# Moving ScalarE's second normalization scaling from slot 3 to slot 5 of a row attention, and its store behind the value-row DMAs

## What is computed

```
projected = einsum('bte,fe->btf', query, in_proj_weight)      # q, k, v of 16 heads of 8
attention = einsum('bhtd,bhkd->bhtk', q / sqrt(8), k) + causal mask
x   = einsum('bhtk,bhkd->bhtd', softmax(attention), v)
out = einsum('bte,fe->btf', x, out_proj_weight)
x   = layernorm(x + out)        # (x - mean) / sqrt(var + 1e-5), no weights
```

## Time and profile before

| | us |
|---|---|
| Median of 3 runs (830.15 to 830.43) | 830.31 |
| The profiled execution, its own time | 829.71 |
| Its span | 828.0 |
| TensorE busy in the span | 577.7 (70%) |
| TensorE weight loads | 391.7 (47%) |
| VectorE | 465.2 (56%) |
| GpSimd | 405.4 (49%) |
| ScalarE | 321.6 (39%) |
| Mean granted TensorE clock | 0.83 of full |

### The profile page before, as it was taken

The page is one execution under the profiler, slowest core; times in us unless marked ns, Lnnn a source line. Parts: engine busy times, 40 slices in busy tenths (PEclk is TensorE's granted clock), DMA queues, the critical chain, the costliest instruction groups (busy, mean ns, idle before and its releaser), DMA issues. The chain is left out here.

```text
span 828.0 us, 16573 instructions
## 1 busy us (share of the span) xinstructions
PE 577.7 (70%) x5632; PEld 391.7 (47%) x5633; DVE 465.2 (56%) x1216; ACT 321.6 (39%) x685; POOL 405.4 (49%) x661
## 2 busy tenths in 40 slices
PE   2769788888888753899928888888411359878910
PEld 1335445445545332899915566656200236555610
DVE  1646666755766326455516899999587622222105
ACT  1035655565556720355514556564300021312105
POOL 7034544544454520544256588863240156777623
PEclk9978989988999955899967999999855556978665
DMA  4674656655530000222221111210100113434217
GB/s 115 139 172 91 144 117 124 125 111 109 108 70 16 15 13 1 58 67 70 55 65 39 40 53 52 68 44 28 51 8 0 41 44 58 86 62 87 23 16 203
DMA packets 72935, 57.69 MB, mean 70 GB/s; under 512 B 15608, under 2 KB 62624, under 8 KB 72864
## 3 DMA queue, kind: packets, MB, share of 16 engines
q1 hardware_dynamic: 64928, 47.72, 24.8%
q0 software_dynamic: 7936, 9.05, 6.3%
HBM read 36.95 MB, written 19.53 MB: 68 GB/s over the span
## 5 line engine op out<-in xcount | busy, mean ns | idle before, releaser
L578 DVE TENSOR_REDUCE a_mx<-a_psR 128x6 f32<-128x768 f32 x128 | 121.8, 954 | 65.6 <-PE a_psR L316 63.9
L245 POOL TENSOR_SCALAR_AFFINE_SELECT a_pr<-a_pr 128x512 f32<-128x512 f32 x128 | 81.3, 635 | 134.8 <-ACT a_pr L492 134.7
L492 ACT ACTIVATE a_pr<-a_psR 128x768 f32<-128x768 f32 x128 | 103.5, 810 | 86.6 <-PE a_psR L329 85.8
L756 POOL DMA_INDIRECT e_xt<-x1d,source x40 | 38.1, 952 | 54.9 <-PE e_psX L767 33.4
L1642 POOL DMA_INDIRECT acc<-e_ot,e_ixa x32 | 50.3, 1572 | 23.3 <-DVE e_ot L1682 11.8
L308 PE MATMUL a_psR<-a_maskA,identb 128*128 128x256 bf16 x256 | 54.0, 296 | 8.6 <-DMA a_ks<-qkd 8.0
L336 PE MATMUL a_psO<-a_pr,a_va 128*32 128x256 f32 x512 | 46.9, 442 | 3.8 <-ACT a_onT L484 2.1
L1707 ACT ACTIVATE e_hT<-e_psH,e_b 128x512 f32<-128x512 f32 x32 | 22.0, 687 | 70.6 <-PE e_psH L1727 69.4
L1743 PE MATMUL e_psY<-e_w,e_hT 128*128 128x128 f32 x256 | 46.6, 338 | 1.9 <-ACT e_hT L1707 1.9
L326 PE MATMUL a_psR<-a_qs,a_ks 50*128 50x256 bf16 x256 | 37.6, 291 | 14.2 <-DMA a_qs<-a_mlo 11.5
L1007 POOL TENSOR_TENSOR a_rs<-a_ve,mhalf 128x2 f32<-128x2 f32 x32 | 22.8, 711 | 47.9 <-DVE a_ve L1255 46.8
(11 more groups left out here) (296 smaller groups left out, 1434.0 us busy)
## 6 DMA issues: line engine op xcount, KB each, us to landing
qkd<-a_hml SPq DMA_DIRECT2D x16, 384.0 KB, 3.0
e_w<-in_fc SPq DMA_DIRECT2D x16, 256.0 KB
a_qs<-qkd SPq DMA_DIRECT2D x32, 96.0 KB
a_ks<-qkd SPq DMA_DIRECT2D x32, 96.0 KB
ys<-e_yt SPq DMA_DIRECT2D x40, 64.0 KB, 1.5
a_qs<-qkd SPq DMA_DIRECT2D x32, 64.0 KB
a_ks<-qkd SPq DMA_DIRECT2D x32, 64.0 KB
x1d<-a_x SPq DMA_DIRECT2D x16, 128.0 KB, 1.8
```

The lines of the kernel that those rows point to most:

```text
L245: g.affine_select(out=diagonal, in_=diagonal, pattern=[[0, 4], [1, 128]], compare_op=ALU.is_ge, fill=0.0, base=0, channel_multiplier=-1).t ...
L492: a.activation(pr[s][:, :, 0:3, :].rearrange("p x k q -> p x (k q)"), psR[:, r:r + 2, 0:384], ACT.Exp).then_inc(probs, 1)
L578: v.tensor_reduce(mx[b % 2][:, :, 2 * u:2 * u + 35:17], psR[:, r:r + 2, 0:384].rearrange("p x (k c) -> p x k c", c=128), AX.X, ALU.max).th ...
L756: pool.indirect_dma_start(xt[n % 4][:], None, x1d, bass.IndirectOffsetOnAxis(ap=source[:, n:n + 1], axis=0)).then_inc(x_in[n % 4], 16)
```

## The change

On ScalarE, the scaling of batch G stands behind the exp of slot 5 instead of slot 3. Within slots 4 and 5 it is thus passed by the copy of the values, the exp of slot 4, `mhi`, `onT` and the exp of slot 5. On SP, the wait for the scaling and the store of `x1` stand behind the four row DMAs and ahead of the stack loads, instead of ahead of the rows. Nothing else changes.

```
--- before.py
+++ after.py
@@ -192,9 +192,6 @@
                     sp.wait_ge(qk_high, P + 1)
                     sp.wait_ge(qk_low, P + 1)
                     sp.dma_start(qkd[P % 2].rearrange("c r f t -> f (c r) t"), hml[P % 2][:]).then_inc(hml_out[P % 2], 16)
-                if G is not None:
-                    sp.wait_ge(x1_sb, G + 1)
-                    sp.dma_start(x1v[G], x1[G % 2][:]).then_inc(x1_out[G % 2], 16)
                 if V is not None:
                     for parts, ready, a in ((mhi, mhi_sb, 0), (mlo, mlo_sb, 1)):
                         sp.wait_ge(ready, V + 1)
@@ -202,6 +199,9 @@
                             r = 64 * h + 48 + a
                             sp.dma_start(qs[V % NQ][r:r + 1], parts[V % 2][:, h, :]
                                          ).then_inc(rows_in[V % NQ], 16)
+                if G is not None:
+                    sp.wait_ge(x1_sb, G + 1)
+                    sp.dma_start(x1v[G], x1[G % 2][:]).then_inc(x1_out[G % 2], 16)
                 if P is not None:
                     sp.wait_ge(hml_out[P % 2], 16 * (P // 2 + 1))
                     if P >= NQ:
@@ -491,7 +491,7 @@
                         r = banks(probs, (B, s))
                         a.activation(pr[s][:, :, 0:3, :].rearrange("p x k q -> p x (k q)"), psR[:, r:r + 2, 0:384], ACT.Exp
                                      ).then_inc(probs, 1)
-                    if s == 3 and G is not None:
+                    if s == 5 and G is not None:
                         act.wait_ge(nr_sb, G + 1)
                         if G >= 2:
                             act.wait_ge(x1_out[G % 2], 16 * (G // 2))
```

## The result

| | Before | After |
|---|---|---|
| Median, us | 830.23 (827.54 to 830.43, now 4 runs) | 786.9 (783.59 to 788.36, 4 runs) |
| Profiled execution, us | 829.71 | 785.63 |
| Span, us | 828.0 | 783.8 |
| TensorE busy | 577.7 (70%) | 559.3 (71%) |
| Mean granted TensorE clock | 0.83 | 0.845 |

The ratio is 0.9489, with a 95% interval of 0.9452 to 0.9527. The direction was right, the size was not. The predicted gain was 33.9 us, the measured one 43.3 (44.2 between the two profiled spans). In the later runs on two chips it was 36.5 and 39.3.

What follows compares the result with a forecast made beforehand. It took TensorE to bound each step, stalled at L347 by the chain from POOL's `nr` through ScalarE's scaling. 28.0 + 11.8 - 7.1 + 1.2 = 33.9 us off 829.71 gave 795.8, plus 0.60 for the median: 796.4, range 790 to 806.

Steps and rivals of the forecast that it cites:

- Item 1: TensorE's transposes of the row maxima (L347), 13 steps: with the scaling out of slot 3 the whole stall goes, 28.0 us.
- Item 2: TensorE's clock in the attention steps: without the stalls it stays up, 8 falls of 1.48 us saved, 11.8 us.
- Rival A: Attention steps: the clock still falls because TensorE idles a little in every step; price 11.8, giving 808.2 us; chance 0.12.
- Item 3: Slot 5: TensorE's first weighing of values (L336) becomes late, waiting for POOL's mask and `onT`; 0.62 a step, 7.1 us cost.
- Items 4 to 6: Scaling's new place in slot 5, SP's row DMAs, SP's stack loads and preloads: each claimed to cost 0.
- rival C: SP's row DMAs come a little late, 0.8 in 10 to 12 steps, giving 804 to 806 us; chance 0.14.
- item 5: SP's row DMAs: they never waited for the store, so moving it saves nothing; rows still land in time, cost 0.
- Item 7: The drain, steps 15 to 17: the 1.64 wait for `onT` in step 15 shrinks, 1.2 us gained; steps 16 and 17 give 0.
- Item 8: Later stages with unchanged code: low-clock stretches begin elsewhere, about 1.5 us each; two allowed with either sign, taken as 0.
- B: Slot 5 costs nothing because TensorE's delay may vanish in VectorE's stretch from slot 0 to 4; 789.3 us; chance 0.11.
- D: First exp scores of slot 0: row DMAs become the bound and the kernel gets slower, 847 to 848 us; chance 0.03.
- E: The copy of the values is late for another reason, so the change does nothing and all stays at 830; chance 0.02.

## Why the prediction was wrong where it was

**Item 1, the stall: right.** 28.0 us of waits at L347 became 0.3, and the transposes come at T. The runs with `nr` early show that the cause was the chain, and the run with the store alone that nothing else in the diff touches it.

**Item 2, the clock in the steps: right.** All eight falls are gone; the clock is 1.00 from 81.65 to 203.16 and from there to the drain. Rival A falls with it. Its condition was met twice over, by idles of 0.6 in 13 steps and of up to 1.4 in 13 steps, and the clock was at 1.00 in the steps 2 to 11 of both kernels. The depth-cycling that the Trainium skill describes (page "TensorE: Matmul & The Clock Gate", section "A second HAM failure mode: psum-queue depth-cycling") isn't seen in these steps. But the ground on which item 2 stood was less firm than it looked. It took the clock to stay up with stalls of up to 1.7, from the one of 1.70 in step 14. The same stall was followed by 3.5 us at 0.50 in the run with only the drain changed, and by 10.4 in the run with the store alone. The forecast for the steps came true; that the profile showed this stall without a fall was luck.

**Item 3, slot 5: right in place and size.** L336 waits 0.61 for L245, at T + 1.91 where T + 1.80 was forecast, with `onT` at T + 1.43 (forecast 1.37). The steps are 13.44 (forecast 13.4). The wait occurs 11 times where ten were expected. Moving `nr` behind the mask takes out 0.44 a step and leaves 0.2 for `onT` (the item had 0.3), which shows both of the item's releasers.

**Items 4 to 6: right, with one exception.** The scaling ends at T + 2.92 (forecast 3.0) and nobody waits for it. The rows cost nothing in eight of the nine steps. In step 3 a wait of 0.8 is rival C's, in one step where C had 10 to 12. That step took 14.26 and the next one 13.13, which is 0.5 of the 0.9 by which steps 2 to 11 ran above the forecast. It is no accident of one execution: the same step took 13.86 and 14.12 in the other two profiles of the changed kernel, and it is the one of 18.17 with the scaling in slot 6. SP was slower than the rows I had read. In step 7 its last two row DMAs take 2.35 to issue (in the changed kernel the rows stand in L200 and the store in L204):

```profile
...
150.59 1.15 SPq L200 DMA_DIRECT2D a_qs<-a_mhi  x2
151.78 2.35 SPq L200 DMA_DIRECT2D a_qs<-a_mlo  x2
154.18 0.58 SPq L204 DMA_DIRECT2D x1d<-a_x  x1
...
159.95 0.43 SPq L1854 DMA_DIRECT2D pjs<-in_pj  x1
```

The last preload ends at 160.38, T + 11.0 and not 10.1. The cover was large enough. What item 5 said of the store's place ("leaving its place saves nothing") is true in the old order only; in the new one it is worth 14.1 us, as the run with the scaling alone shows. The sum didn't need that number, since both halves move together.

**Item 7, the drain: this is the step that failed.** It read the wait of 1.64 in step 15 and gave it its length alone: "1.2 us gained". It was the first part of the loss. The clock fell 1.3 us behind that wait and stayed at 0.50 to the end of the attention, the 19.7 us from 290.00 to 309.70 above. With item 7's 1.2 and the 1.4 of step 14 the drain was to take 31.8; it took 27.30. Item 2 priced the clock in the steps, where the mean of the earlier trace rows showed it, and its window of 51.10 us at 1.00 ended at 290.00, just where the low stretch begins. One more window, from 290 to the routing, would have shown 0.50, and that this wait had a low stretch behind it as the others had, only far longer than their 3.4 us. The runs show that moving the scaling in the drain gives this clock back; why it falls where it does stays open. With the 4.5 in place the point would have been 791.9, 5.0 above the result, and the range moved with it would have held 786.9.

**Item 8, the unchanged code: mis-sized.** I allowed 3 us on either side for the later stages and nothing for the start. The profile from which I forecast has the highest T2 (84.20) and a rest (518.3) near the upper end of 15. After the change they were 2.55 and 3.9 lower, and the kernel before run again was 3.1 and 5.6 lower without any change. This is 6.4 of the 10.1 us by which the profiled parts lie below the forecast (9.5 in the medians), and the runs give no sign that the change has a part in it. In the later runs the gain is 36.5 and 39.3 us (ratios 0.9545 and 0.9521) rather than 43.3, and the 4.5 of the drain are about what lies above 33.9.

**Rivals B to E.** B (slot 5 costs nothing, 789.3) is nearest in time and wrong in its mechanism: the 0.6 is there in 11 waits. D and E have nothing for them. The sign was never in doubt; the range failed because its lower end came from B and not from the spread of the rest.

What stays open: why the start and the later stages differ by 4 and 9 us between executions of one kernel. The runs show the spread, not its cause. The clock is at most a part of it: the rests of 518.3 and 512.7 of the kernel before had mean clocks of 0.79 and 0.81, but the changed kernel run again took 512.4 at 0.79.

## What to carry to other kernels

An instruction that waits in an in-order queue also holds all that stands behind it. Place it behind those whose input is ready and for whom others wait, and move its own followers on the next queue too: here one half of the change brought 24 to 26 us of the stretch by itself, the other nothing by itself and 14 more with the first. Then work out who releases the engine next; this was exact to 0.1 us from the rows of one step. Ask of every wait, in the drain as in the steps, which clock the engine has behind it, and ask it of more than one execution. And set the width of a forecast by how far two executions of the same kernel lie apart, part by part, before the change is argued at all.

## What the runs showed of the hardware

- The length of a wait doesn't settle by itself whether TensorE's clock falls. In the steps, stalls of 2.3 to 2.4 were followed by 1.2 GHz in eight of ten, waits of 0.6 (with `nr` early) and of 1.4 (scaling in slot 4) never. With only the scaling moved, a wait of 1.33 for the rows (until 232.74) was followed by some 3.4 us at 0.50, and one of 1.37 (until 191.01) was not.
- The stall of 1.70 in step 14 left the clock up in both profiles of the kernel before, and was followed by 3.5 and by 10.4 us at 0.50 in two runs with the same code up to there on TensorE and ScalarE. In the drain a wait of 1.64 or 1.65 went with 0.50 for some 20 us or more, and one of 0.61 was followed by 10.5 us at a mean of 0.51.
- A fall in a step cost 1.48 us; the one in the drain, where the clock didn't come back before the end of the attention, cost about 5.6 (34.09 against 27.30, less 1.2 of waiting).
- Executions of one kernel on one core spread over 816 to 831 us across chips and runs, from stretches that the change never touches, while the stretch from T2 to routing repeated within 0.4 us in three profiles of the changed kernel (in two of the kernel before it took 225.5 and 227.4).
- SP's issue of four small row DMAs took 2.4 us in some steps and 3.5 in the one shown, and landing took 1.6 to 3.2 there.
